# Pooling of the last batch by blocks of 128 tokens, with the other blocks' weights in one 68-row product

## What is computed

```python
h = gelu(x @ fc1_w.T + fc1_b)
x = x + concat([h @ fc2_w.T + fc2_b, h @ experts_w[idx].T + experts_b[idx]])
scores = tanh(x @ W1 + b1) @ v                       # one per token
mask = l <= j   if type == 0                         # tokens up to j
       l >= j   if type == 1                         # tokens from j on
       l != j   if type == 2                         # all but j
p = softmax(where(mask, scores[l], -1e30))           # over l, for each j
x = x + (p @ x) / count(mask)
```

## Time and profile before

| | us |
|---|---|
| median of 3 runs | 1351.5 |
| lowest and highest of these | 1351.4, 1351.54 |
| the profiled execution, its time | 1351.54 |
| its span in the profile | 1349.8 |
| TensorE busy | 1343.3 |
| VectorE busy | 1244.2 |
| ScalarE busy | 877.4 |
| POOL busy | 7.4 |

### The profile page before, as it was taken

One profiled execution on the slowest core, in us unless ns is written; L12 is line 12 of the kernel. 1 busy time (PEld: TensorE's weight loads), 2 busy tenths in 40 slices (PEclk: granted clock), 3 DMA queues, 4 the chain that ended last, 5 costly groups with the idle time before them and its releaser, 6 DMA issues.

```text
span 1349.8 us, 22079 instructions
## 1 busy us (share of the span) xinstructions
PE 1343.3 (100%) x8749; PEld 873.0 (65%) x8749; DVE 1244.2 (92%) x2068; ACT 877.4 (65%) x1509; POOL 7.4 (1%) x12
## 2 busy tenths in 40 slices
PE   9999999999999999999999999999999999999998
PEld 4458476584856748476584766748567584765856
DVE  7988899999999999999999999999999999999997
ACT  4868748376693856848477583756938478484763
POOL 0000000000000000000000000000000000000001
PEclk9999999999999999999999999999999999999999
DMA  8410020110202102011110201102011020200015
GB/s 293 149 48 24 1 75 21 52 44 1 79 17 63 32 8 79 9 63 32 35 61 1 79 17 55 40 0 79 17 63 32 8 79 9 69 26 15 27 24 103
DMA packets 30488, 65.07 MB, mean 48 GB/s; under 512 B 6194, under 2 KB 7986, under 8 KB 27954
## 3 DMA queue, kind: packets, MB, share of 16 engines
q1 hardware_dynamic: 28802, 61.05, 13.8%
q0 software_dynamic: 1152, 2.09, 1.2%
q10 hardware_dynamic: 432, 0.53, 0.1%
HBM read 44.79 MB, written 18.87 MB: 47 GB/s over the span
## 4 chain that ended last, share of the span: by engine, by line
PE 99%; DMA 0%; DVE 0%; ACT 0%; ACTq 0%; issue 0%
PE ps L416 16%; PE ps L418 16%; PE ps L417 16%; PE ps L335 14%; PE ps L336 14%; PE ps L337 14%; PE ps L448 1%; PE ps L306 1%; PE ps L621 1%; PE ps L317 1%; PE ps L321 1%; PE ps L319 1%; PE ps L444 1%; PE ps L442 1%; PE ps L443 1%; DMA xr<-in_xT 0%
## 5 line engine op out<-in xcount | busy, mean ns | idle before, releaser
L418 PE MATMUL ps<-hl,w2h 128*128 128x512 f16 x768 | 291.0, 379 | 0.0
L417 PE MATMUL ps<-hh,w2h 128*128 128x512 f16 x768 | 291.0, 379 | 0.0
L416 PE MATMUL ps<-hh,w2l 128*128 128x512 f16 x768 | 291.0, 379 | 0.0
L336 PE MATMUL ps<-xl,w1h 128*128 128x256 f16 x960 | 261.7, 273 | 0.0
L335 PE MATMUL ps<-xh,w1h 128*128 128x256 f16 x960 | 261.7, 273 | 0.0
L337 PE MATMUL ps<-xh,w1l 128*128 128x256 f16 x960 | 261.7, 273 | 0.0
L673 ACT ACTIVATE g<-ps,b1s,ds 128x512 f32<-128x512 f32 x240 | 173.4, 773 | 97.6 <-PE ps L337 84.4
L335 PE MATMUL ps<-xh,ch 128*128 128x256 f16 x720 | 196.4, 273 | 0.0
L337 PE MATMUL ps<-xh,cl 128*128 128x256 f16 x720 | 196.2, 273 | 0.0
L336 PE MATMUL ps<-xl,ch 128*128 128x256 f16 x720 | 196.2, 273 | 0.0
L1092 DVE SCALAR_TENSOR_TENSOR hl<-g,ix,hh 128x512 f16<-128x512 f32 x244 | 178.2, 743 | 3.1
(11 more groups left out here) (227 smaller groups left out, 2369.3 us busy)
## 6 DMA issues: line engine op xcount, KB each, us to landing
xr<-in_xT SPq DMA_DIRECT2D x62, 256.0 KB, 3.1
er<-in_ew SPq DMA_DIRECT2D x15, 1024.0 KB, 5.7
out<-xr SPq DMA_DIRECT2D x60, 256.0 KB, 2.4
raw<-in_w SPq DMA_DIRECT2D x28, 256.0 KB, 6.3
er<-in_w SPq DMA_DIRECT2D x3, 1024.0 KB, 9.8
out<-sums POOLq DMA_DIRECT2D x8, 255.5 KB, 5.0
xr<-in_ew SPq DMA_DIRECT2D x1, 1024.0 KB, 5.9
out<-er SPq DMA_DIRECT2D x3, 256.0 KB, 2.4
```

The lines of the kernel that those rows point to most:

```text
L336: mm(to, wh, ml, start=False, stop=False, skip_group_check=True)
L416: mm(po(b, o), wl, hh[:, k, :], start=False, stop=False, skip_group_check=True)
L417: mm(po(b, o), wh, hh[:, k, :], start=False, stop=False, skip_group_check=True)
L418: m = mm(po(b, o), wh, hl[:, k, :], start=False, stop=k == NH - 1, skip_group_check=True)
```

## The change

In the new pooling each token's own block of 128 tokens and the other three blocks are treated apart.

- **Own block.** For block t the weights of its own 128 tokens, `own[:, block t]`, are made exact in fp32 (`own_distance`, `own_weights`), and one fp32 product per piece multiplies them with `xn` (`own_tokens`). `unseen`, made by `see`, is now one 128x128 tile for all blocks.
- **Other blocks.** `peaks` takes each block's highest score, `rel` is score minus it, and `parts` its exponential. `block_sums` multiplies these weights with `xn`: four fp32 products with 68 output rows, of which rows 0 to 3, 32 to 35 and 64 to 67 hold the same sums of blocks 0 to 3 (the columns of `part` between them are zero). `block_arg` holds for each of these rows and each token j how far the block's peak lies under j's maximum, or a huge number where j must not see the block (`places` prepares which row is which block, and which block reaches where); `block_weights` makes exp of it, `block_e` rounded and `block_w` exact. With `block_low` in rows 0 to 3 and the low part of the sums in rows 32 to 35, one single-pass product of 68 rows per piece (`other_blocks`) adds all that the other blocks contribute.
- **Totals.** `weights(t)`: for each block two one-column products, one from `block_w` and the blocks' sums of weights `zsums`, one from `own`.
- **Order.** The first half's backward scan, its maxima over the first half and its peaks now come before the wait for the second half's scores; half of chunk 3 is transposed, and two of the four score columns are made, before the last fc2 products. `nh`, `nl`, `ph`, `pl`, `natural_low`, `negative`, `weight_low`, the 17 products and two loads of ScalarE's tables are gone. Three `natural_low` stood among the steps of batch 14's pooling; the 12 operations of `places` stand there now.

```diff
@@ -145,16 +146,33 @@
...
+    PIECES = ((0, slice(0, S), pf[2]), (1, slice(0, S), pa), (2, slice(0, S), po(LAST, 2)),
+              (3, HALVES[0], pf[3]), (3, HALVES[1], pf[0]))
...
+    own = row[0]
+    score_cols, zsum, zcol = po(LAST, 1)[:, 0:4], pf[1][0:4, 8:9], (po(LAST, 1)[:, 16:18], pf[1][:, 16:18])
...
@@ -476,17 +496,17 @@
...
+        def natural_up(c, n, halves=(0, 1)):
...
@@ -499,7 +519,52 @@
...
+            if v:
+                e.wait_ge(xn_done, 2)
+                e.wait_ge(rel_done, 1)
             mm(pf[n][:, 0:HALF], avs[:, :], att[:, HALVES[v]], start=True, stop=True).then_inc(score_done)
+            for t in (2 * v, 2 * v + 1):
+                m = mm(score_cols[:, t:t + 1], att[:, of_block(t)], avs[:, 0:1], start=True, stop=True)
+            m.then_inc(cols_done)
+
+        def block_sums(v):
+
+            e.wait_ge(part_done, v + 1)
+            e.wait_ge(xn_done, KD + v)
+            e.wait_ge(fifth_copied, nth_pair(LAST, PAIRS - 1))
+            for t in (2 * v, 2 * v + 1):
+                m = mm(bank[7][0:ROWS3, :], part[:, t * ROWS3:(t + 1) * ROWS3], xn[:, t, :], start=t == 0, stop=t == 3)
+            if v:
+                m.then_inc(sums_done)
...
+        def own_tokens(n):
+
+            t, d, to = PIECES[n]
+            e.wait_ge(own_p_done, t + 1)
+            e.wait_ge(xn_done, KD + 1)
...
+            mm(to[:, d], own[:, of_block(t)], xn[:, t, d], start=True, stop=False, skip_group_check=True)
+
+        def weights(t):
+
+            e.wait_ge(block_w_done, t // 2 + 1)
+            e.wait_ge(sums_kept, 1)
+            mm(zcol[t // 2][:, t % 2:t % 2 + 1], block_w[0:4, of_block(t)], zsums, start=True, stop=False, skip_group_check=True)
+            e.wait_ge(own_p_done, t + 1)
+            m = mm(zcol[t // 2][:, t % 2:t % 2 + 1], own[:, of_block(t)], ones[:, :], start=False, stop=True, skip_group_check=True)
+            if t % 2:
+                m.then_inc(z_done)
+
+        def other_blocks(n):
+
+            t, d, to = PIECES[n]
+            e.wait_ge(r_low_done, 1)
+            e.wait_ge(e_low_done, t // 2 + 1)
+            mm(to[:, d], block_e[0:ROWS3, of_block(t)], block_r[0:ROWS3, d], start=False, stop=True,
+               skip_group_check=True).then_inc(piece_done)
@@ -588,56 +653,36 @@
...
         natural_up(2, 2)
+        e.wait_ge(xn_done, 1)
+        natural_up(3, 0, (0,))
...
         attend_half(1)
-        e.wait_ge(nl_done, 1)
-        natural_up(3, 0)
-        e.wait_ge(nl_done, 2)
+        e.wait_ge(xn_done, KD)
+        natural_up(3, 0, (1,))
         score_half(1, 1)
-        for v in (0, 1):
...
-        for _ in range(17):
-            mm(bank[7], eh[:, 0, :], hh[:, 0, :], start=True, stop=True)
...
+        block_sums(0)
+        block_sums(1)
+        e.wait_ge(part_done, 3)
+        e.wait_ge(own_done, 2)
+        mm(zsum, ecol, ones[:, :], start=True, stop=True).then_inc(z_done)
+        own_tokens(0)
+        own_tokens(1)
+        weights(0)
+        weights(1)
+        other_blocks(0)
+        other_blocks(1)
+        own_tokens(2)
+        own_tokens(3)
+        own_tokens(4)
+        weights(2)
+        weights(3)
+        other_blocks(2)
+        other_blocks(3)
+        other_blocks(4)
 
...
-            eng.preload_act_table(ACT.Gelu)
+            if b < LAST - 1:
+                eng.preload_act_table(ACT.Gelu)
...
@@ -995,32 +1037,55 @@
...
+        natural_copy(2, 2)
+        natural_copy(3, 0, slice(0, 2))
...
+        natural_copy(3, 0, slice(2, 4))
...
+        def parts(v):
+
+            e.wait_ge(rel_done, v + 1)
+            act(part[:, :].rearrange("p (t s) -> p t s", s=69)[:, blocks_of(v), 0:65:32],
+                rel[:, blocks_of(v)].rearrange("p (t s) -> p t s", s=1).broadcast_to([P, 2, 3]), ACT.Exp).then_inc(part_done)
+
+        def own_weights(t):
+            e.wait_ge(neg_done, t // 2 + 1)
+            e.wait_ge(scol_done, 1)
+            act(own[:, of_block(t)], own[:, of_block(t)], ACT.Exp, bias=scol[:, t:t + 1], scale=-1.0).then_inc(own_p_done)
+
+        def block_weights(v):
+
+            e.wait_ge(arg_done, v + 1)
+            act(block_e[0:ROWS3, HALVES[v]], block_arg[0:ROWS3, HALVES[v]], ACT.Exp, scale=-1.0)
+            act(block_w[0:4, HALVES[v]], block_arg[0:4, HALVES[v]], ACT.Exp, scale=-1.0).then_inc(block_w_done)
...
+        parts(0)
+        parts(1)
         own_scores(1, 1)
-        eng.preload_act_table(ACT.Exp)
...
+        e.wait_ge(cols_done, 2)
+        act(scol[:, :], score_cols, ACT.Copy).then_inc(scol_done)
+        act(ecol, rel, ACT.Exp).then_inc(part_done)
+        own_weights(0)
+        own_weights(1)
+        block_weights(0)
+        e.wait_ge(z_done, 1)
+        act(zsums, zsum, ACT.Copy).then_inc(sums_kept)
+        e.wait_ge(sums_done, 1)
+        act(block_r[0:ROWS3, :], bank[7][0:ROWS3, :], ACT.Copy).then_inc(sums_kept)
+        own_weights(2)
+        own_weights(3)
+        block_weights(1)
...
@@ -1515,71 +1580,122 @@
...
+        def places():
...
+            eng.memset(part[:, :], 0.0).then_inc(tail_small)
+            ts(thrice, io[0:ROWS3, 0:96].rearrange("p (k u) -> p k u", k=3)[:, :, 0:4], lcol[0:ROWS3, 0:1], None,
+               ALU.is_equal).then_inc(tail_small)
...
+            add(block_of, thrice.rearrange("p k u -> p u k")).then_inc(tail_small)
...
+            tt(block_n, block_of, first, ALU.mult).then_inc(tail_small)
+            add(is_block, block_of).then_inc(tail_small)
...
+            add(block_id, block_n).then_inc(tail_small)
+            ts(open_f, cF[0:ROWS3, i], BIG, is_block, ALU.add, ALU.mult).then_inc(tail_small)
+            ts(open_b, cB[0:ROWS3, i], BIG, is_block, ALU.add, ALU.mult).then_inc(tail_small)
...
+            ts(reach, first, block_id, open_f, ALU.is_gt, ALU.mult).then_inc(tail_small)
+            ts(reach_b, first, block_id, open_b, ALU.is_lt, ALU.mult).then_inc(tail_small)
...
+            stt(reach, reach, -BIG, reach_b, ALU.add, ALU.add).then_inc(tail_small)
+            ts(rz[:, :], lcol[:, :], cntq[:, i], cntp[:, i], ALU.mult, ALU.add).then_inc(tail_small)
+
+        def peaks(v, n):
+
+            eng.tensor_reduce(peak[:, blocks_of(v)], in_two(n[:, 0:HALF]), AX.X, ALU.max).then_inc(peak_step)
+            e.wait_ge(cols_done, v + 1)
+            e.wait_ge(peak_step, v + 1)
+            tt(rel[:, blocks_of(v)], score_cols[:, blocks_of(v)], peak[:, blocks_of(v)], ALU.subtract).then_inc(rel_done)
...
+        def own_distance(v, steps):
+            e.wait_ge(tail_max, steps)
+            e.wait_ge(seen, 2)
+            tt(in_two(own[:, HALVES[v]]), unseen[:, :].rearrange("p (a b) -> p a b", a=1).broadcast_to([P, 2, P]),
+               in_two(mt[:, HALVES[v]]), ALU.add).then_inc(neg_done)
...
+        def block_distance(v):
+            e.wait_ge(bias_step, 3)
+            tt(in_two(block_arg[0:ROWS3, HALVES[v]]), in_two(mt[0:ROWS3, HALVES[v]]),
+               peak_of[:, blocks_of(v)].rearrange("p (a b) -> p a b", b=1).broadcast_to([ROWS3, 2, P]),
+               ALU.subtract).then_inc(arg_done)
...
+        def block_low(v):
+            e.wait_ge(block_w_done, v + 1)
+            tt(block_e[0:4, HALVES[v]], block_w[0:4, HALVES[v]], block_e[0:4, HALVES[v]].bitcast(f32),
+               ALU.subtract).then_inc(e_low_done)
+
+        def normalizers(v):
+            e.wait_ge(z_done, v + 2)
+            e.wait_ge(tail_small, 12)
+            tt(rz[:, blocks_of(v)], zcol[v], rz[:, blocks_of(v)], ALU.mult).then_inc(rz_step)
+            e.wait_ge(rz_step, 2 * v + 1)
+            eng.reciprocal(rz[:, blocks_of(v)], rz[:, blocks_of(v)]).then_inc(rz_step)
+
+        def output(n):
+            t, d, to = PIECES[n]
+            e.wait_ge(piece_done, n + 1)
+            e.wait_ge(rz_step, 2 * (t // 2) + 2)
+            stt(xn[:, t, d], to[:, d], rz[:, t:t + 1], xn[:, t, d], ALU.mult, ALU.add).then_inc(out_ready)
+
...
-        natural_low(0, 0)
...
-        natural_low(1, 1)
-        pool(3 + 4 + 3 + 4)
-        natural_low(2, 2)
-        pool(2)
+        pool(3 + 4)
+        places()
+        pool(3 + 4 + 2)
         e.wait_ge(score_done, LAST + 1)
         e.wait_ge(own_done, 1)
         scan(mF[:, 1:1 + HALF], pad, pf[3][:, 0:HALF], -BIG, ALU.max, ALU.max).then_inc(scan_step)
+        peaks(0, pf[3])
+        scan(back_of(mB[:, 0:HALF]), pad, back_of(pf[3][:, 0:HALF]), -BIG, ALU.max, ALU.max).then_inc(scan_step)
+        e.wait_ge(scan_step, 1)
+        stt(mt[:, 0:HALF], mFx[:, 0:HALF], cF[:, i], sc[:, 0:HALF], ALU.add, ALU.max).then_inc(tail_max)
+        e.wait_ge(tail_max, 1)
+        e.wait_ge(scan_step, 2)
+        stt(mt[:, 0:HALF - 1], mB[:, 1:HALF], cB[:, i], mt[:, 0:HALF - 1], ALU.add, ALU.max).then_inc(tail_max)
         e.wait_ge(score_done, LAST + 2)
-        e.wait_ge(scan_step, 1)
         scan(mF[:, 1 + HALF:1 + S], pad, pf[1][:, 0:HALF], mF[:, HALF:HALF + 1], ALU.max, ALU.max).then_inc(scan_step)
         scan(back_of(mB[:, HALF:S]), pad, back_of(pf[1][:, 0:HALF]), -BIG, ALU.max, ALU.max).then_inc(scan_step)
...
```

(28 more changed lines are left out.)

175 lines of the change are left out of this document (53 added, 122 removed).

## The result

The changed kernel takes 1347.84 us (median of 11 runs, 1347.53 to 1348.76), the kernel before 1351.46 in the runs beside it. The ratio is 0.9974, with a 95% interval of 0.9965 to 0.9982: 3.6 us less, where 4.3 were forecast. The time lies in the stated range (1345.9 to 1349.6). The profiled execution took 1347.95 us with a span of 1346.2, so 1.75 lie around the span, as before.

What follows compares the result with a forecast made beforehand. After the last fc2 products, VectorE, then TensorE's pooling products bound the end. Won 1.53 + 4.68, lost 1.60, stores 0.3 more: net 4.3 off 1351.5 gives 1347.2 us, range 1345.9 to 1349.6.

Steps and rivals of the forecast that it cites:

- The first scan: VectorE, first half: 1.83 us of natural_low go, 2.40 us of places() come, so the scan moves from 1327.01 to 1327.58.
- The second half's scores: TensorE's last scores, delayed by 0.85 us of work moved ahead, readable at 1329.93, before VectorE asks at 1330.52.
- The 0.59: Time in us by which the second half's scores are ready before VectorE asks; the most that cheaper small steps could win.
- The release: VectorE's second-half scans and ScalarE's parts(1) let TensorE start the last block sums at 1332.80 instead of 1334.33: 1.53 us won.
- TensorE's run: TensorE's products from parts(1) to the last column: 7.42 us, readable after 7.63 against 12.31 before, 4.68 won.
- Waits in the run: Four places where TensorE's products need ScalarE or VectorE results; all due before wanted, thinnest slack 0.4 us.
- rival (a): Hand-overs between engines in the new tail cost more, 1.6 + 1.0 us: 1349.8 us; chance 0.14.
- Behind the products: After the last column, VectorE's normalisers and three outputs take 2.10 us, 1.60 lost; the last stores add 0.3.
- The sum: Terms 1.53 + 4.68 - 1.60 = 4.61 us, net gain 4.3 after the stores: span 1345.5 us, time 1347.2 us.
- rival (b): Without the 17 filler products TensorE's clock falls from 2.4 to 1.2 GHz before the run and stays: 1355.6 us; chance 0.05.
- Rival (c): POOL's accumulating stores, forecast to land at 1342.4, are delayed and end last: 1348 to 1350 us; chance 0.04 with the like.

Runs made afterwards that it cites:

- the transposition experiment: The changed kernel with the half of chunk 3's transposition ahead of the last fc2 products moved behind them: 1347.96 us.
- the light `places()`: The changed kernel with 9 of the 12 operations of places() moved behind the release of the block sums: 1347.90 us.
- The run without fillers: The kernel before without its 17 products of which nothing is read: 1354.01 us, ratio 1.0017.

## Why the prediction was right, step by step

- **The first scan.** Forecast 1327.58, and 1327.50 in the timeline, from which the 1327.01 of before were taken: close only because two errors nearly cancel. The 12 operations of `places()` in VectorE's timeline:

```profile
1319.04 0.29 DVE L1592 MEMSET part<- 128x276 f32 x1
...
1321.06 0.68 DVE L1369 TENSOR_TENSOR sums<-sums,raw 128x511 f32<-128x511 f32 x1
```

  From the first to the row behind the last it is 2.02 us, 0.17 each, and not 2.40. With 2.02 the sum would be 1327.20, and this is where the scan stands in the profile of the transposition experiment, whose head on VectorE is the same. The profiled execution of the changed kernel is 0.3 us late from further up (its mark at 1319.04, there at 1318.74).
- **The second half's scores.** This premise failed. Forecast readable at 1329.93, 0.59 before VectorE asks. Their product starts at 1329.46; in the run with the light `places()`, where VectorE waits for them, its scan starts 0.74 behind the product's start (1329.18 to 1329.92) and not 0.64, so they were readable at 1330.20. VectorE asked at 1330.20 instead of 1330.52, since the steps before it were shorter than their nearest rows (the reduction 0.33 against 0.45). The 0.59 is gone, 0.27 of it by the scores and 0.32 by VectorE: the two stand side by side, and VectorE alone does not set the pace. The transposition moved, and the light `places()`, showed both walls.
- **The release.** Forecast 1332.80, measured 1332.40, 1.93 us won instead of 1.53: the small steps again, although the profile is 0.3 us late. The early maxima were worth 1.5 us, by the run that undid them.
- **TensorE's run.** This is the term that was mis-sized: forecast 7.42 us to the last column, measured 8.75. By kind: block sums 1.93 (forecast 1.72), the 4-row sum 0.12 (0.20), own tokens of blocks 0 and 1 1.91 (1.72), columns 1.24 (0.79), 68-row products 0.57 (0.48), own tokens of blocks 2 and 3 1.72 (1.72), columns 1.24 (0.79). The columns are 0.90 of the 1.33 too many, and with 128 rows in all columns the last output stands 0.91 us nearer to the release (1332.00 to 1341.87, against 1332.40 to 1343.18). The step that failed took L639's price, where eight passes of one form follow each other, for a sequence that alternates between 4 and 128 weight rows. Of the two wide groups of 0.2 each, the own tokens have 0.09 from the same change, since the pass ahead of the 4-row column takes 0.52 us from start to start instead of 0.43. The other 0.1 is in their first pass, behind the 4-row sum, which in turn counts 0.12 instead of 0.20. In the block sums the first pass, behind the wait, takes 0.48 and the last, ahead of the 4-row sum, 0.52. That sum's weights have 128 rows and 4 columns, so it is not a matter of rows there; the cause is open. That an fp32 product with 68 output rows costs what one with 128 does was right: 0.43 a pass.
- **Waits in the run.** None, as forecast; every signal was there in time, and TensorE was busy throughout. So rival (a), dear hand-overs, did not come; what the forecast lacked was the price of a change of form, which no rival had.
- **Behind the products.** Forecast 0.21 + 2.10 us from the last column to the last output's end, measured 2.03 (1341.15 to 1343.18). The store and the closing took 3.02 instead of 2.66, where 0.3 more was forecast.
- **The sum.** 0.40 won at the release, 1.33 lost in the run, 0.28 won behind it, 0.06 lost in the store: 0.7 more than the forecast span of 1345.5, so 1346.2. That the time came within 0.7 us of the forecast is in part luck: half of what the run lost came back by steps of VectorE that were priced too high.
- **The clock, rival (b).** It did not come in the changed kernel: mean clock 0.998 or more in all runs. But the argument against it was weak. A gap of 0.63 us that did no harm was taken as a sign that the fillers were cover and cost nothing to lose; without them the kernel before loses 2.5 us. What most likely saves the changed kernel is that the first block sums, wide products, stand where the fillers stood; that was argued from the rows and not tried. The Trainium skill, "TensorE: Matmul & The Clock Gate", section "Part 1: The HAM clock gate", says that the throttled clock is the default and that sustained work is needed to leave it. The run without fillers agrees: 0.50 from 1334 on, with TensorE at work again, and back only in 1340 to 1342. The changed kernel, whose longest rest from 1327 to 1341 is 0.66 us, does not contradict it.
- **Rival (c)**, POOL's transfers: its last issue came at 1337.07. With the median of 5.3 us from issue to landing on this profile's page it lands near 1342.4 by estimate, before the last output is even computed (1343.18).

## What to carry to other kernels

Price a short product by its neighbours, not by its shape alone: a change between 4 weight rows and more from one product to the next cost about 0.1 us here, as much as the one-column pass itself, and sorting by form gave most of it back. Before products that seem to do nothing are taken out, or narrow ones are moved together, look at what holds the clock in that place: it stayed up behind wide products here and fell behind one-column passes. Where a release has two causes within a tenth of a microsecond, take both away at once; each alone shows nothing. And before two traces are compared, line them up at an instruction ahead of the edit.
